# A scan over two neighbouring states in one instruction, and the step-times-input products made ahead

## The reference

```python
dA = exp(dt * A)                         # A: channel x state
state = state * dA + (dt * u) * B        # over 512 time steps
y = sum over the 16 states of state * C
out = (y + D * u) * silu(layernorm(x))   # added to x, turned to rows
```

## Time and profile before

| what | before |
|---|---|
| median of 3 runs | 1061.68 us (1059.53 to 1061.94) |
| the profiled execution: time, span | 1053.36 us, 1051.6 us |
| busy PE / DVE / ACT / POOL | 899.8 / 828.9 / 517.5 / 753.6 us |
| recurrence stage, from the first to the last scan's start | 104.8 to 574.6 us |
| mean granted PE clock | 0.924 of full speed |

### The profile page before, as it was taken

How to read it: one execution, slowest core, us unless ns; L and a number is a source line. 1 busy time by engine, 2 the same in 40 slices (tenths; PEclk the granted TensorE clock), 3 DMA queues, 4 the chain that set the end, 5 groups by cost and what they waited for, 6 DMA issues and landing times.

```text
span 1051.6 us, 16598 instructions
## 1 busy us (share of the span) xinstructions
PE 899.8 (86%) x4352; PEld 653.7 (62%) x4353; DVE 828.9 (79%) x1349; ACT 517.5 (49%) x959; POOL 753.6 (72%) x482
## 2 busy tenths in 40 slices
PE   5876655689999789988999999869999999998993
PEld 2222334566665456655665555649998999887992
DVE  4788999999999899989999216768798989898000
ACT  3777634445655465555665222115554555454541
POOL 2436889899999799989993111027989888877872
PEclk9997656789999999999999989889999999999996
DMA  5568922562228322562210230134676777675432
GB/s 175 195 263 308 341 64 78 209 210 81 81 74 330 117 80 80 209 230 80 80 60 30 75 128 11 65 125 141 173 226 187 217 189 218 159 228 100 77 56 35
DMA packets 69987, 152.14 MB, mean 145 GB/s; under 512 B 7585, under 2 KB 23969, under 8 KB 64306
## 3 DMA queue, kind: packets, MB, share of 16 engines
q1 hardware_dynamic: 59410, 126.97, 35.2%
q0 software_dynamic: 10528, 24.65, 11.9%
HBM read 112.80 MB, written 38.80 MB: 144 GB/s over the span
## 4 chain that ended last, share of the span: by engine, by line
DVE 41%; PE 29%; issue 19%; DMA 3%; ACT 2%; DVEq 2%; POOL 1%; SPq 0%; POOLq 0%; ACTq 0%
DVE bank L1344 8%; PE bank L665 6%; DVE gs L1358 6%; PE bank L684 5%; DVE e_gu_lo L1571 4%; DVE e_gu_hi L1570 4%; PE bank L769 3%; PE bank L611 3%; PE bank L771 3%; DVE bank L1563 3%; PE bank L770 3%; DVE p_acc L1286 3%; DVE e_dn_lo L1571 2%; DVE e_dn_hi L1570 2%; DVE h_p L1344 2%
## 5 line engine op out<-in xcount | busy, mean ns | idle before, releaser
L1151 POOL TENSOR_TENSOR dbu<-bcs,m_w 128x2048 f32<-128x2048 f32 x64 | 296.1, 4627 | 11.4 <-DVE bank L1344 8.6
L925 ACT ACTIVATE bank<-m_dt,c_a 128x512 f32<-128x512 f32 x256 | 171.0, 686 | 196.8 <-DVE gs L1358 196.7
L1344 DVE TENSOR_TENSOR_SCAN bank<-bank,dbu 128x512 f32<-128x512 f32 x192 | 229.0, 1213 | 14.6 <-ACT bank L925 10.5
L611 PE MATMUL bank<-ident,gs 128*128 128x128 f32 x768 | 135.2, 307 | 70.0 <-DVE gs L1358 63.0
L665 PE MATMUL bank<-ws_gu,f_xnT 128*128 128x352 f32 x576 | 191.9, 474 | 2.8 <-ACT f_hT L947 1.9
L611 PEld LDWEIGHTS bank<-ident,gs 128*128 128x128 f32 x768 | 95.3, 154 | 129.5 <-DVE gs L1358 107.3
L665 PEld LDWEIGHTS bank<-ws_gu,f_xnT 128*128 128x128 f32 x576 | 106.2, 196 | 50.5 <-issue 5.3
L769 PE MATMUL bank<-e_gu_hi,e_xT_hi 128*128 x376 | 130.0, 346 | 4.0 <-DVEq L1585 3.1
L1358 DVE TENSOR_TENSOR gs<-bank,bcs 128x512 f32<-128x512 f32 x192 | 126.5, 665 | 0.0
L771 PE MATMUL bank<-e_gu_hi,e_xT_lo 128*128 x376 | 121.8, 324 | 0.0
L770 PE MATMUL bank<-e_gu_lo,e_xT_hi 128*128 x376 | 121.7, 324 | 0.0
(11 more groups left out here) (166 smaller groups left out, 1683.8 us busy)
## 6 DMA issues: line engine op xcount, KB each, us to landing
bcs<-bc_scratch SPq DMA_DIRECT2D x32, 1024.0 KB, 8.8
e_gu<-in_wgu SPq DMA_DIRECT2D x16, 1408.0 KB, 8.9
e_dn<-in_wdn SPq DMA_DIRECT2D x16, 512.0 KB
out_rows<-xt SPq DMA_DIRECT2D x18, 256.0 KB, 2.1
p_x<-in_x SPq DMA_DIRECT2D x4, 1024.0 KB, 7.0
u_scratch<-p_u SPq DMA_DIRECT2D x4, 1024.0 KB, 3.9
silu_z_scratch<-p_sz SPq DMA_DIRECT2D x4, 1024.0 KB, 5.0
dt_scratch<-p_dt SPq DMA_DIRECT2D x4, 1024.0 KB, 4.2
```

The source lines that it names most:

```text
L611: last = mm(Y[:, t * P:(t + 1) * P], tile[:, t * P:(t + 1) * P], ident[:], is_transpose=True, start=first and t == 0, stop=final and t == ...
L925: f(HS[k % RING_H][:], m_dt[:, q % 2, :], ACT.Exp, scale=c_a[:, q, n:n + 1]).then_inc(exp_done, 1)
L1151: g.tensor_tensor(part_, Bs[:, gr * GRP:(gr + 1) * GRP, :], w, ALU.mult).then_inc(dbu_ready, 1)
L1344: v.tensor_tensor_scan(to, h, dbu[:, n, :], 0.0, ALU.mult, ALU.add).then_inc(scan_done, 1)
```

## The change

Two neighbouring states 2p and 2p+1 become a pair. PSUM is one tensor of eight banks, and `PAIR` = banks 0 and 1, or banks 6 and 7, by turns. One DVE instruction scans 1024 columns; so that the second state starts from zero, ACT writes 0 into its first decay with a one-column Copy. One DVE instruction multiplies the pair by C. In the new order the product of a pair comes right behind its scan, unless something else stands between. The states that POOL multiplies by C are two pairs, (2, 3) and (10, 11). Only slot 0 keeps the old form.

The expert row bank `YO` moves to bank 2, `take_y` works in place in `Y`, and PE's first tile of a slot waits for `gated` in place of `take_y`. `xn_turn` writes to `YO`. The product dt * u is made by POOL in the first stage (batches 0 and 1), in slot 0 (batch 2) and in slot 2 (batch 3), stored by SP, and loaded per slot by one more DMA into one of two `m_w` tiles. `stats` is split in three, with other work between the parts. The tables of places are new.

```diff
-POOL_N = (1, 5, 9, 13)
+POOL_N = (2, 3, 10, 11)
-ORDER = (0, 2, 3, 1, 4, 6, 7, 5, 8, 10, 11, 9, 12, 14, 15, 13)
+ORDER = (0, 1, 4, 5, 2, 3, 6, 7, 8, 9, 12, 13, 10, 11, 14, 15)
-PE_AT = (3, 3, 4, 4, 5, 5, 6, 6, 7, 7, 8, 8, 9, 9, 9, 10, 10)
-LATE_AT = (0, 0, 0, 1, 1, 2, 2, 3, 3, 5, 5, 6, 6, 6, 6, 6, 6)
-XN_TURN_AT = (12, 9)
-GATE_AT, HT_AT, XN_AT, XNT_AT = (6, 8), 2, (14, 10), (15, 15)
-TAKE_AT, LOGITS_AT, GATED_AT, HIDDEN_AT, STATS_AT, ADD_AT = 2, 5, 4, (9, 13), (8, 1), 15
+PE_AT = (4, 4, 4, 4, 4, 4, 4, 5, 6, 7, 8, 8, 9, 9, 9, 9, 10)
+LATE_AT = (0, 1, 2, 3, 4, 5, 6, 6, 6, 6, 6, 6, 6, 6, 6, 6, 6)
+XN_TURN_AT = (12, 11)
+GATE_AT, HT_AT, XN_AT, XNT_AT = (5, 7), 1, (14, 10), (15, 15)
+LOGITS_AT, HIDDEN_AT, STATS_AT, ADD_AT = 3, (5, 6), (4, 0), 13
...
+        PAIR = (banks[:, 0:2, :], banks[:, 6:8, :])
...
+                sp.dma_start(m_w[par][:, 0, :], w_d[bass.ds(b, 1), :, q, :]...).then_inc(w_loaded[par], 16)
...
                 if m == 0 and not (isinstance(i, int) and i < 1):
-                    pe.wait_ge(y_taken, i)
+                    pe.wait_ge(x1_ready, i)
...
+                if n % 2 == 0:
...
+                    f(PAIR[p % 2][:, 0, :], m_dt[:, q % 2, :], ACT.Exp, scale=c_a[:, q, n:n + 1]).then_inc(exp_done, 1)
+                else:
+                    f(PAIR[p % 2][:, 1, 0:1], zero[:], ACT.Copy)
+                    f(PAIR[p % 2][:, 1, 1:L], m_dt[:, q % 2, 1:L], ACT.Exp, scale=c_a[:, q, n:n + 1]).then_inc(exp_done, 1)
...
-                g.tensor_tensor(m_w[:, 0, :], m_u[:, q % 2, :], m_dt[:, q % 2, :], ALU.mult).then_inc(w_ready, 1)
...
+            def scan_pair(b, q, p):
...
+                v.tensor_tensor_scan(to, h, w, 0.0, ALU.mult, ALU.add).then_inc(scan_done, 2)
...
+            def pair_times_c(b, q, p):
...
+                v.tensor_tensor(gs[:, g:g + 2, :], PAIR[p % 2], Cs[:, n:n + 2, :], ALU.mult).then_inc(g_ready, 2)
...
+                for p in range(PAIRS):
+                    scan_pair(b, q, p)
+                    if not rows and p == 0:
+                        take_y(*past)
+                    if rows and p == STATS_AT[q > 0]:
+                        stats(j, b - 1)
...
                     for c in range(2):
-                        if n == HIDDEN_AT[c]:
+                        if p == HIDDEN_AT[c]:
...
+                    if 2 * p in DVE_N:
+                        pair_times_c(b, q, p)
+                    if rows and p == 0:
+                        take_y(*past)
+                    if rows and p == STATS_AT[q > 0]:
+                        spread(j)
+                    if p == 0:
+                        gated(*past)
```

More of the change, by code:

```diff
@@ L186, in program @@
         g_p = msb("g_p", [P, RING_P, L])
+        m_w.append(msb("m_w1", [P, 1, L]))
         slots.close()
@@ L1019, in xnT_of @@
             def xnT_of(q):
-                xnT_copy((first + q, q), first + q - 1)
+                xnT_copy((first + q, q), first + q - 1, TP)
             xn_of(0)
@@ L1149, in slot @@
                     part_ = dbu[:, gr * GRP:(gr + 1) * GRP, :]
-                    w = m_w[:, 0:1, :].to_broadcast([P, GRP, L])
+                    w = m_w[q % 2][:, 0:1, :].to_broadcast([P, GRP, L])
                     g.tensor_tensor(part_, Bs[:, gr * GRP:(gr + 1) * GRP, :], w, ALU.mult).then_inc(dbu_ready, 1)
+                    if isinstance(b, int) and i == 0 and gr == 1:
+                        for k in range(DT):
+                            products(B - 2, k)
+                    if isinstance(b, int) and b == 0 and q == 2:
+                        products(B - 1, gr)
                     if rows and gr == SWISH_AFTER:
@@ L1398, in clear, with slot_by_state @@
                 dve.wait_ge(bc_stored, 16 * B)
+                dve.wait_ge(u_stored, 16 * B)
+                dve.wait_ge(w_stored, 16 * B)
                 v.memset(xt[:, 2:4, :], 0.0)
                 v.memset(f_xnT[:, 2:4, :], 0.0).then_inc(dummy_ready, 1)
+            def slot_by_state():
+                for n in range(NS):
+                    scan(n)
+                    if n == SOFT_AT:
+                        for k in range(DT):
+                            soft(B - 1, k)
+                    if n in GAP_AT:
+                        gap(B - 1, GAP_AT.index(n))
+                    if n - 1 in GAP_AT:
+                        total(B - 1, GAP_AT.index(n - 1))
+                    if n and n - 1 in DVE_N:
+                        times_c(n - 1)
+                times_c(NS - 1)
@@ L1402, in slot @@
             def slot(b, q, rows):
                 i = b * DT + q
-                later = not (isinstance(b, int) and b == 0 and q == 0)
                 j = ((b - 1) * DT + q, q)
-                for n in range(NS):
-                    scan(b, q, n)
-                    if isinstance(b, int) and b == 0:
-                        if q == 0 and n == SOFT_AT:
-                            for k in range(DT):
-                                soft(B - 1, k)
-                        if q == 0 and n in GAP_AT:
-                            gap(B - 1, GAP_AT.index(n))
-                        if q == 0 and n - 1 in GAP_AT:
-                            total(B - 1, GAP_AT.index(n - 1))
-                        if q == 2 and n == CLEAR_AT:
-                            clear()
-                    if n and n - 1 in DVE_N:
-                        times_c(b, q, n - 1)
-                    if n == TAKE_AT and later:
-                        take_y(*((b, i - 1, q - 1) if q else (b - 1, i - 1, DT - 1)), i - DT if rows else 0)
-                    if n == GATED_AT and later:
-                        gated(*((b, i - 1, q - 1) if q else (b - 1, i - 1, DT - 1)))
+                past = (b, i - 1, q - 1) if q else (b - 1, i - 1, DT - 1)
@@ L1424, in slot @@
+                for p in range(PAIRS):
[4 more added lines that the diff above has]
+                        stats(j, b - 1)
+                    if not rows and q == 2 and 2 * p == CLEAR_AT:
+                        clear()
                     for c in range(2):
-                        if n == HIDDEN_AT[c]:
+                        if p == HIDDEN_AT[c]:
                             if rows:
@@ L1429, in slot @@
                                 hidden((0, 0), c)
-                    if rows:
-                        if n == STATS_AT[q > 0]:
-                            stats(j, b - 1)
-                times_c(b, q, NS - 1)
-            for q in range(DT):
+                    if 2 * p in DVE_N:
[3 more added lines that the diff above has]
+                    if rows and p == STATS_AT[q > 0]:
+                        spread(j)
+                    if p == 0:
+                        gated(*past)
+                    if rows and q and p == STATS_AT[1]:
+                        variance(j)
+                    if rows and q == 0 and p == STATS_AT[0] + 1:
+                        variance(j)
+            slot_by_state()
+            for q in range(1, DT):
                 slot(0, q, False)
@@ L1450, in _ @@
             for q in range(TB - 1):
-                stats((first + q, q), B - 1)
+                row_stats((first + q, q))
             whole((first + 1, 1))
-            stats((NT - 1, TB - 1), B - 1)
+            row_stats((NT - 1, TB - 1))
             whole((first + 2, 2))
```

217 lines of the change are left out of this document (136 added, 81 removed).

## The result

| | before | after |
|---|---|---|
| median | 1060.61 us (1057.89 to 1061.94, 4 runs) | 1075.54 us (1073.16 to 1081.24, 4 runs) |
| ratio, 95% interval | | 1.0154 [1.0115, 1.0193] |
| profiled execution: time, span | 1053.36, 1051.6 us | 1081.24, 1079.5 us |
| recurrence stage ends at (last `take_y`) | 578.4 us | 596.9 us |
| from there to the end of the span | 473.2 us | 482.6 us |

The change makes the kernel 1.5% slower. So I read the stage of the recurrence alone, where the end moved by 18.4 us.

The account below looks back on a forecast made before the run. DVE sets the pace, PE nearly as full; late PE results would lengthen slots. Terms +7.8, +2.4, +3.6, -4.7 and +1.0 make +10.1 us on 1061.7: 1072 us, own range 1066 to 1080, widened to 1051 to 1080.

Parts of the forecast that it names:

- PE's lateness: Full slots: PE starts tile 2 only at 10.9 us, up half ready at 24.1, so second `hidden` waits 1.7 us.
- ACT behind `xnT_copy`: Start of next slot: first decays stand behind `xnT_copy` and PE's `xn_turn`, so DVE waits 0.5 us more.
- POOL, SP, `m_w`: Products dt * u made ahead, stored and loaded: off the path, cost 0, up to 5 us if cover is gone.
- The wait for x: First slots of later batches: DVE's wait for rows of x goes, since `stats` comes later, -4.7 us.
- DVE's own list: Full slots: DVE alone would need 27.3 us a slot, 0.95 less than now.
- The clock: Rival: PE drops to 1.2 GHz in one slot in four, 1090 us or more; 0.05, shared with first stage beyond 1080.
- The turn of the loop: After q = 3: DVE's unexplained 4.07 us stall stays, and the wait for ACT's copy hides under it.
- Slots 0 to 3: Slots 1 to 3: DVE saves 0.2 us each, but waits 1.4 us once for slot 1's first exponentials; sum +1.0.
- DVE stays the bound: Rival: PE's stretch is at least 1.7 us shorter, no `hidden` waits; -11, 1051 us; chance 0.24.
- pairs arriving in lumps: Full slots: pairs reach PE late and in lumps, and `hidden` comes at scan 6 of 7; DVE waits 1.7 us.

Follow-up runs that it names:

- e3: The kernel after with only `xn_turn` moved ahead of tiles 10 and 9 (`XN_TURN_AT` 10, 9 for 12, 11): 1062.81 us, ratio 1.0042.
- e4: The kernel after with dt * u made by POOL in every slot, no products made ahead, stored or loaded: 1073.74 us, ratio 1.0165.
- e8: e5 with dt * u made by POOL in the slot, no products made ahead, stored or loaded: 1046.38 us, ratio 0.9899.
- e5: The kernel after with `hidden` at pairs (6, 7) and `xn_turn` at places (10, 9): 1043.08 us, ratio 0.9877.
- e12: e5 with 20 semaphore-only DVE increments behind each scan of pairs 0 to 5, 480 in the loop's body: 1051.90 us, ratio 0.9928.
- e9: e6 with `hidden` behind scans 13 and 15 in place of 9 and 13: 1055.25 us, ratio 0.9974.
- e7: e1 with 30 more semaphore-only DVE instructions in each full slot, 120 in the loop's body: 1046.83 us, ratio 0.9887.
- e1: The kernel after with `hidden` at pairs (6, 7) in place of (5, 6): 1045.30 us, ratio 0.9907.
- e11: The kernel after with two more up pieces ahead of tile 2 and `xn_turn` at (10, 9), `hidden` left at (5, 6): 1048.38 us, ratio 0.9906.
- e6: The single-state kernel before with the new `PE_AT` and `LATE_AT` and the new place of the router logits: 1090.18 us, ratio 1.0295.
- e10: The kernel after with the old `PE_AT` and `LATE_AT` of the kernel before: 1122.36 us, ratio 1.0613.

## Why the prediction was right

The time, the sign and the mechanism came out as forecast (1075.5 us for 1072, in the range of 1066 to 1080). Step by step, with waits counted from the end of an instruction's hold, 0.09 us more than its idle row:

- **PE's lateness: right.** Tile 2 can start at +11.1 us into the slot (predicted 10.9), the second up half is ready 13.2 us later (13.2), at +24.35 (24.1). Two waits of `hidden` share the delay, 0.52 and 1.05 = 1.57 us (1.7 in one).
- **ACT behind `xnT_copy`: right**, 0.51 us for 0.5, the Copy 0.09 us for 0.1. e3 takes it away alone. (The terms printed for this path, 27.6 + 0.48 + 1.3 + 0.1, make 29.48 and not 29.55.) After q = 3, where it was to hide under the loop's stall, it shows as well, 0.47 and 0.46 us of idle rows, since that stall is gone.
- **POOL, SP, `m_w`: right**, zero (e4, e8).
- **The wait for x: right**, gone.
- **DVE's own list: mis-sized.** Predicted 27.3 us a slot; slot 6 without its waits needs 30.03 - 1.57 - 0.51 = 27.95. The pair scan holds 2.20 us, not 2.17 (8 x 0.03); the product 1.14, not 1.11 (6 x 0.03); and a product behind its own scan starts 2.37 us after it, 0.17 later than another instruction would, not 0.12 (4 x 0.05): 0.62 in all. e5, where the last product has `hidden` between it and its scan, has one such wait less and 27.72. Against 28.25 before, pairs save DVE 0.3 to 0.5 us, not 0.95: 3.6 us over 12 slots and not 11.4.
- **The clock: not in the sum.** I had it as a rival, with one slot in four dropping for its whole 13 us. It was one in three, but for 3 us each: 1.54 + 1.68 + 1.70 + 1.68 = 6.6 us.
- **The turn of the loop: missed.** I let the 4 us stay; both stalls go, -7.0 us. That a long DVE body brings them is shown by e12, and single states keep them (e9). That it was the shorter body of the pairs that took them away is the likely reading, and not shown: e7 records more DVE instructions a round (361) than the kernel before (340) and has no stall.
- **Slots 0 to 3**: +2.6 us for +1.0. Of these 1.5 us are that slot 0 starts at 106.3 and not at 104.8, which says little: in the 14 profiles it starts anywhere from 104.8 to 106.9. The 1.60 us of waiting ahead of slot 1 came as foreseen, and slots 1 to 3 are 0.2 to 0.5 us longer, not shorter.

In a sum for slots 4 to 15: `hidden` 21.5 and ACT 5.9 us of idle rows plus 0.09 for each of 33 waits make +30.4; DVE's own saving -3.6, x -4.7, the turns -7.0: +15.1, measured +16.0 (364.97 against 348.95 us between the `take_y` of slots 3 and 15). Predicted were 9.1. The two large errors, a saving that was not there and a stall that went, cancel in part. So the close hit in the time is partly luck: the stage as a whole grew by 18.4 us where 10.1 were forecast, and the medians by 14.9.

The rivals: "DVE stays the bound" was wrong of after and right of e1, e5 and e11, which is where its time lies (1043 to 1048). And one statement of mine was too simple: I laid the lateness to pairs arriving in lumps. What the runs show is three things that must fit each other:

| scans | tables | `hidden` | ratio |
|---|---|---|---|
| single | old | 9, 13 | 1 |
| single | new | 9, 13 | 1.0295 |
| single | new | 13, 15 | 0.9974 |
| pairs | old | 5, 6 | 1.0613 |
| pairs | new | 5, 6 (after) | 1.0154 |
| pairs | new | 6, 7 | 0.9907 |
| pairs | new, `xn_turn` early | 6, 7 | 0.9877 |

Here "tables" are `PE_AT` and `LATE_AT`; the single kernels keep the other places of before (with `LOGITS_AT` of after where the tables are new), the pair kernels those of after. The new tables need a late `hidden` with either scan. With pairs and the other places of after the old tables are far worse (1.0613 against 1.0154), through ACT's copy of the rows; pairs with the old tables and that copy at its old place were not run, so what the tables alone are worth to pairs is open. With everything in its place, pairs and their order bring 0.7% (0.9974 to 0.9907), mostly by the two stalls and the waits for x.

## What to carry to other kernels

Merging instructions on the engine that sets the pace gains the fixed part of each, but coarsens its results: walk through the in-order engine behind it and look where it stands idle, and whose result is then asked for first; moving one consumer by a pair was worth 2.5%, the merging with all that came along with it 0.7%. Check every consumer of a reordered list, not only the last (e6), and those on a third engine too (e10: ACT's copy). An instruction merged with its successor also loses the one that stood between producer and reader.

## What the hardware showed

- **A loop whose body is too long stalls at its turn.** 2.3 to 4.6 us of DVE at each turn in the single-state kernels (2.26 and 2.39 in e6) and in e12, none in the other pair kernels, e7 with 120 increments more among them; from 370 to 510 us 5 to 8 packets of the instruction queue against 0. How long is too long was not found (e7). The Trainium skill (Runtime: NRT & Kernel Launch, "Instruction fetch mechanics") says that a taken branch whose target isn't in the window held must wait for its code to come by DMA. These runs agree, and put 2.3 to 4.6 us on it.
- **Instructions that only count a semaphore were free** behind a scan, 20 in a row (0.093 us from one to the next, 1.9 us in all, beside a scan of 2.2): e12's slots of q = 1 and 2 last 27.72 us, as e5's.
- **A dependent instruction pays 0.17 us more** on 1024 columns (2.37 against 2.20 us from the scan's start). The Trainium skill (VectorE: DVE Perf Modes, "The DRAIN you can't avoid") has a semaphore between two cost nothing extra; here, as in the earlier trace rows, it does not hold. The same section adds, which the prediction left out, that a next instruction that is not held starts earlier, and the rows without a wait fit that.
- **TensorE's granted clock and idle gaps.** In after it fell behind gaps of 2.29, 2.30, 1.79 and 1.85 us ahead of tile 2, and did not behind one of 2.29 us (at 515.50) and ones of 1.80 to 1.86 us in the other full slots. So the gap alone does not decide it, and what does was not settled; from slot 5 on e1 and e3 show no fall, but e7, with e1's order on PE, does in four slots, behind gaps of 2.06 to 2.87 us. That an order is safe from it was therefore not shown.
